# Cross-attention on one core: the raw context loaded as two column halves, each behind its own half of o, and issued ahead of the turn's store

## What is computed

```python
def layer(emb, latent, Wq, bq, Wk, bk, Wv, bv, gamma, beta):   # (32,224,512), (32,750,256)
    q = jnp.einsum('bte,ef->btf', emb, Wq) + bq
    k = jnp.einsum('bml,le->bme', latent, Wk) + bk
    v = jnp.einsum('bml,le->bme', latent, Wv) + bv
    w = jnp.einsum('bte,bme->btm', q, k) / sqrt(512)
    w = jax.nn.softmax(w, axis=1)                               # over the 224 rows t
    x = jnp.einsum('btm,bme->bte', w, v) + emb
    mu, var = mean(x, -1), var(x, -1)
    return (x - mu) * rsqrt(var + 1e-6) * gamma + beta
x = layer(x, ctx_512, L0 weights)
x = layer(x, ctx_512, L1 weights)
```

## Time and profile before

| | before |
|---|---|
| median of 3 runs | 1096.07 us |
| the profiled execution, its own time | 1094.51 us |
| its span, first to last instruction | 1092.7 us |
| PE matmul busy | 1024.3 us (94%) |
| PE weight load busy | 951.3 us (87%) |
| DVE busy | 869.1 us (80%) |
| ACT / POOL busy | 664.5 us (61%) / 564.8 us (52%) |
| mean granted TensorE clock | 0.974 |
| moved by DMA | 99.58 MB, 367054 packets, 91 GB/s |

### The profile page before, as it was taken

One profiled execution on the slowest core, in us unless ns is written; L12 is line 12 of the kernel. 1 busy time (PEld: TensorE's weight loads), 2 busy tenths in 40 slices (PEclk: granted clock), 3 DMA queues, 4 the chain that ended last, 5 costly groups with the idle time before them and its releaser, 6 DMA issues.

```text
span 1092.7 us, 24724 instructions
## 1 busy us (share of the span) xinstructions
PE 1024.3 (94%) x6984; PEld 951.3 (87%) x6984; DVE 869.1 (80%) x2593; ACT 664.5 (61%) x1873; POOL 564.8 (52%) x519
## 2 busy tenths in 40 slices
PE   6797999999999999999999999999999999999984
PEld 5677989988899898989989998989989899899973
DVE  2456888788888988888888888888888888888863
ACT  1325677566666765666667666666676566666743
POOL 0013465655546556555565565555655655456654
PEclk8688999999999999999999999999999999999997
DMA  7734344444444344443444444444444444344101
GB/s 144 169 78 82 78 95 96 90 93 93 89 97 100 92 95 84 99 102 76 100 98 93 91 89 97 96 83 98 100 93 94 83 101 104 78 102 98 46 18 34
DMA packets 367054, 99.58 MB, mean 91 GB/s; under 512 B 324833, under 2 KB 350881, under 8 KB 367009
## 3 DMA queue, kind: packets, MB, share of 16 engines
q1 hardware_dynamic: 364368, 99.02, 41.2%
q10 hardware_dynamic: 2640, 0.01, 0.2%
HBM read 84.29 MB, written 14.68 MB: 91 GB/s over the span
## 4 chain that ended last, share of the span: by engine, by line
PE 51%; DMA 17%; SPq 16%; issue 7%; DVE 3%; ACT 3%; POOL 2%; DVEq 0%; ACTq 0%; POOLq 0%
PE oq_bank L591 21%; DMA raw<-in_ctx_dram 14%; SPq L346 9%; SPq L347 5%; PE score_bank L567 4%; PE score_bank L568 4%; PE score_bank L572 4%; PE pv_bank L622 3%; DMA cb<-in_ctx_dram 3%; PE oq_bank L543 2%; PE oq_bank L538 2%; PE oq_bank L539 2%; PE pv_bank L618 2%; PE pv_bank L617 2%; ACT probs L749 2%
## 5 line engine op out<-in xcount | busy, mean ns | idle before, releaser
L591 PE MATMUL oq_bank<-probs,raw 125*128 125x224 f32 x1536 | 320.8, 359 | 21.9 <-DMA raw<-in_ctx_dram 16.6
L591 PEld LDWEIGHTS oq_bank<-probs,raw 125*128 125x128 f32 x1536 | 284.8, 193 | 29.9 <-DMA raw<-in_ctx_dram 22.0
L749 ACT ACTIVATE probs<-probs,neg_max 125x224 f32<-125x224 f32 x384 | 181.5, 476 | 178.4 <-DVE neg_max L959 178.3
L1142 POOL TENSOR_TENSOR psum<-probs 125x672 f32<-125x672 f32 x64 | 103.3, 1614 | 300.2 <-ACT probs L758 300.2
L567 PE MATMUL score_bank<-qT_hi,cT_hi 128*125 128x224 f32 x768 | 199.2, 286 | 3.1 <-ACT cT_hi L706 1.6
L568 PE MATMUL score_bank<-qT_hi,cT_lo 128*125 128x224 f32 x768 | 189.1, 273 | 0.0
L1185 POOL TENSOR_TENSOR y_out<-z,gamma_row 112x512 f32<-112x512 f32 x63 | 94.1, 1515 | 160.3 <-ACT z L782 160.3
L758 ACT ACTIVATE probs<-probs,rsum 125x224 f32<-125x224 f32 x384 | 154.0, 474 | 22.6 <-DVE rsum L967 22.6
L567 PEld LDWEIGHTS score_bank<-qT_hi,cT_hi 128*125 128x125 f32 x768 | 145.3, 189 | 9.4 <-issue 4.9
L959 DVE CUSTOM_DVE_ANT_0 probs<-score_bank,d_row 125x224 f32<-125x224 f32 x384 | 139.6, 382 | 15.8 <-PE score_bank L572 13.8
L572 PE MATMUL score_bank<-qT_lo,cT_hi 128*125 128x224 f32 x768 | 146.8, 273 | 0.0
(11 more groups left out here) (96 smaller groups left out, 2083.8 us busy)
## 6 DMA issues: line engine op xcount, KB each, us to landing
raw<-in_ctx_dram SPq DMA_DIRECT2D x32, 750.0 KB
cb<-in_ctx_dram SPq DMA_DIRECT2D x256, 92.0 KB
xb<-in_x_dram SPq DMA_DIRECT2D x512, 28.0 KB, 1.7
x<-in_x_dram SPq DMA_DIRECT2D x32, 448.0 KB, 3.6
out_dram<-y_out SPq DMA_DIRECT2D x31, 448.0 KB, 3.1
y<-in_L_xattn_Wq_dram SPq DMA_DIRECT2D x4, 512.0 KB, 8.3
cb<-in_ctx_dram SPq DMA_DIRECT2D x128, 3.5 KB
x<-in_L_xattn_Wk_dram SPq DMA_DIRECT2D x2, 512.0 KB, 9.8
```

Of the source, the lines that this page charges most:

```text
L591: ins = nc.tensor.matmul(o, raw[0:MP, u.slot, c, cols], probs[0:MP, u.par4, c, :], start=(c == 0), stop=(c == MC - 1))
L749: ins = act.activation(probs[0:MP, u.par4, c, :], probs[0:MP, u.par4, c, :], ACT.Exp, bias=neg_max[0:MP, u.par4, c:c + 1], scale=-1.0, acc ...
L1142: pool.tensor_tensor(psum3[0:MP, :, :], probs[0:MP, u.par4, 0:HALF, :], probs[0:MP, u.par4, HALF:MC, :], ALU.add).then_inc(psum3_done, 1)
```

## The change

The raw context of a batch is loaded by two transfers. Transfer l brings the columns `l*128:(l+1)*128` of every row (750 rows of 512 bytes each, where there were 750 of 1024), waits for the half l of o of b(-1) only, and increments a semaphore of its own. PE waits for half 0 ahead of `o_product(a(+0), 0)` and for half 1 ahead of `o_product(a(+0), 1)`. Both transfers are issued ahead of `store(b(-2))`, where the one of before came behind it.

```diff
-        raw_loaded = [sem("raw_loaded0"), sem("raw_loaded1")]
+        raw_loaded = [[sem("raw_loaded00"), sem("raw_loaded01")], [sem("raw_loaded10"), sem("raw_loaded11")]]
...
-            def load_ctx(u):
+            def load_ctx(u, l):
                 if not u.real:
                     return
                 if u.past(-4):
 
-                    sp.wait_ge(o_ready, u.n(-1, 2))
+                    sp.wait_ge(o_ready, u.n(-1, 2, l - 1))
                     sp.sem_inc(wait_alone, 1)
-                sp.dma_start(raw[0:MP, u.slot], ctx[u.batch()].rearrange("(c p) l -> p c l", c=MC)).then_inc(raw_loaded[u.slot], 16)
+                cols = slice(l * P, (l + 1) * P)
+                src = ctx[u.batch()].rearrange("(c p) l -> p c l", c=MC)
+                sp.dma_start(raw[0:MP, u.slot, :, cols], src[:, :, cols]).then_inc(raw_loaded[u.slot][l], 16)
...
-            load_ctx(start)
+            load_ctx(start, 0)
+            load_ctx(start, 1)
...
                 if a(+1).later(1):
                     load_x(a(+1))
+                if a(+0).later(0):
+                    load_ctx(a(+0), 0)
+                    load_ctx(a(+0), 1)
                 store(b(-2))
-                if a(+0).later(0):
-                    load_ctx(a(+0))
...
                 cols = slice(l * P, (l + 1) * P)
-                if u.layer == 0 and l == 0:
-                    pe.wait_ge(raw_loaded[u.slot], u.turns(16))
+                if u.layer == 0:
+                    pe.wait_ge(raw_loaded[u.slot][l], u.turns(16))
```

## The result

| | before | changed |
|---|---|---|
| median of 4 runs | 1096.28 us | 1054.16 us |
| lowest to highest | 1094.2 to 1100.38 | 1051.85 to 1057.63 |
| ratio, 95% interval | 1 | 0.9596 (0.9567 to 0.9625) |
| the profiled execution, time / span | 1094.51 / 1092.7 us | 1051.85 / 1049.8 us |
| mean granted TensorE clock in it | 0.974 | 0.979 |

The change is worth 42 us at the medians, where 30 were forecast. Run again later, beside fresh runs of the kernel before, the same kernel had a ratio of 0.9646 (0.9627 to 0.9665), 38 us.

What follows compares the result with a forecast made beforehand. PE bounds the kernel, with the raw load causing both its winnable stalls; 0.75 us for the raw wait plus 1.3 for earlier cb per pair, over 14.5 pairs, gives 30 us: 1064.5 profiled, 1066 us median, range 1053 to 1096.

Steps and rivals of the forecast that it cites:

- What bounds the kernel: PE, busy 1024.3 of 1092.7 us; its raw wait (21.3 us) and oT_lo wait at L622 (16.3) both come from the raw load.
- The raw wait: PE's wait at the first raw-context product: half 0 issued at R - 3.9, both halves in time, 21.3 us gone.
- R: The moment SyncE issues the raw load, or half 1 in the changed kernel; other times are counted from it in us.
- The price of the halves: DMA cost of doubled rows: 27 ns per 512 bytes, 150 rows on each of 5 engines, 4.1 us a half.
- When cb lands: In the DMA queue behind raw load and store: cb 0.55 to 2.05 us earlier, 1.3 taken as the middle.
- the store might only lie in line: Store between half 1 and cb: cb gains up to 2.05 us if not held, 0.55 if it waits the store's 1.5.
- full pace of the cb issues: Sign in SyncE's queue: cb issues back at two in 1.3 us by 6 to 7.3 us after half 1's issue, instead of 7.55.
- The sum: Per pair of turns, 1.3 us in the L622-stalled one plus 0.75 in the other, 2.05; times 14.5 pairs, 30 us.
- the cap: Most that a turn stalled at L622 can gain: 0.59 + 1.21 = 1.8 us; 1.34 a turn on average, 39 us in all.
- Rival B: Store does not hold cb and both PE stalls go: 39 us, 1057 us, or 1053 with pipeline fills; chance 0.25.
- C: Cb lands as late as now, so the raw stall only moves to L622: 3 us gained, 1093 us; chance 0.12.
- D: Slower because row count rules: cb up to 5 us late, up to some 130 us lost, 1123 us at 36 ns; chance 0.13.

Runs made afterwards that it cites:

- the halves together: Two half loads behind the store, both waiting for both halves of o, against the changed kernel's halves moved behind the store: 1120.84 us, 1.0301 of the kernel before.
- the whole load: As a run: the kernel before with its one whole raw load moved ahead of the store: 1125.35 us, ratio 1.0345.
- The quarters: The changed kernel with every half loaded as two quarters, rows of 256 bytes: 1071.29 us, 0.9785 of the kernel before.

## Why the prediction was wrong

**What bounds the kernel: right.** Both stalls led to the raw load. "Removing the raw wait alone would thus mostly move the stall to L622; what counts is when cb lands" is what the halves together showed: 21.3 us of raw wait gone, the stall at oT_lo up from 16.3 to 51.9.

**The raw wait: right.** Half 0 was issued at R - 3.9, as forecast, and the wait is gone in every turn.

**The price of the halves: the step that failed.** "27 ns for 512 bytes" was right as the share of an engine's time: a window of the changed kernel inside half 0 gives 0.36 x 16 / 213 rows per us = 27 ns (109 GB/s are 213 rows of 512 bytes):

```profile
443.00:445.00 2.00, 2.00 (x20) 1.99 (x19) 0.87 (x4) 1.39 (x4) 1.92 (x2) 1.00 0.36 109
```

But I multiplied it by 150 rows on each of **5** engines, while the same share of 0.36 x 16 counts 5.8 engines as busy. The rows pass at the measured rate, 5 / 213 per us = 23.5 ns on five engines. For the whole load I had taken the rate (750 KB at 121 GB/s, 6.35 us), for the halves the share; by one measure a half is 3.5 us and not 4.1. The Trainium skill's rule of 3 fixed cycles a descriptor besides one per 32 bytes ("DMA: Bandwidth & Descriptors", on why small descriptors are slow), applied to the whole load's 42 ns a row (121 GB/s on five engines), gives an estimated 23 ns for 512 bytes; the trace agrees (23.5).

**When cb lands: mis-sized through it.** With 3.5, half 1 ends at R + 1.65 + 3.5 = R + 5.15 instead of R + 5.95, and cb is 0.8 us earlier. The forecast's 0.55 to 2.05 becomes 1.35 to 2.85, and the measured gain at the last cb issue, 1.6 to 2.3 us (2.1 in the means), lies inside. "The middle, 1.3" fell short of the 1.8 at which the stalled turns stop gaining. The other assumption of that step, that the store might only lie in line, was too kind: with the whole load it held cb by 1.3 of its 1.5 us, with the halves by some 1 us.

The quarters are close to the case that the forecast had worked out: at their rate a half takes 4.2 us, for the 4.1 assumed. There cb came 0.9 us earlier, within 0.55 to 2.05, the stall at oT_lo stayed, and the forecast's sum with that gain, (0.9 + 0.75) x 14.5 = 24 us, stands against 0.81 x 29 = 23.5 measured. So this run bears out the rest of the working, and the size of the half is what failed.

One sign was off beyond that: full pace of the cb issues was to come back at R + 6 to 7.3 and came back at R + 3.65, when half 1 was by this working still under way. From there the 12 issues, held by nothing, take 8.85 us and set when cb is complete: in the five kernels where VectorE waits for cb, the hand-over comes 1.2 to 1.4 us after the last issue's end. That SyncE is held until the raw load has nearly drained fits the kernel before; why it was let go so early here stays open.

**The sum.** With the cap reached a stalled turn gains 1.8, and a pair 1.8 + 0.75 = 2.55, 37 us: measured 37.7. That they agree so well is partly luck: 3.4 us at oT_lo are still there in the window, 0.3 us in one turn of two, and 1.8 us of "issue", which was to stay, went with the rest. Rival B, to which I gave 0.25, described what happened, though its reason did not hold (the store does hold cb) and a small rest of the second stall is left. Its price was 1057, and 1053 with the pipeline fills.

**The range.** Its low end was B's best value with no room for the spread of the runs. The first 100 us vary by 5 us with the clock granted there, and the measured value slipped under it by 1 us. The interval of the ratio, 1048.6 to 1055.0 on 1096.07, reaches into the range, and the second measurement, 0.9646, gives 1057.3, inside it. So the 1 us is chance, but the forecast gain isn't made right by it: 37.7 us in the steady part for 30.

**The rivals C and D** did not come about, but their mechanism is real: with the halves together cb came 0.6 to 0.8 us later, and the kernel was 31 us slower, some 12 of them through the clock. Halving the rows was affordable because half 0 starts 3.9 us early; without that it loses.

## What to carry to other kernels

A load whose wait looks small (0.75 us a turn) can cost as much again through what is queued behind it on the same engines: follow the issue times of the next transfers, not only the waiting instruction. Before splitting or hurrying a load, look at its rate: 121 GB/s at a share of a third says that most engines don't take part, and cutting 125 partitions into 112 and 13 gave the same gain without any new order. When costing pieces of a transfer, use one measure for whole and part; the share and the rate differ by 15% for the rows of 512 bytes.

## What was not expected of the hardware

- The share of busy time counted for rows on five engines grows as they shorten: 0.34 at 1024 bytes, 0.36 at 512, 0.40 at 256, at 121, 109 and 91 GB/s. Quartering the rows costs a quarter of the rate.
- SyncE is held at an issue when a long raw load on five engines is still under way, though the mean share of all 16 is only 0.34 to 0.36: the store's issue took 2.20 us instead of 0.35, a pair of cb issues 3.92 instead of 0.93.
- After stalls of 2.3 to 2.8 us PE was granted 1.2 GHz for 3.5 us in eight turns of the kernel with the halves together, and in other turns with a stall as long it was not. A turn with the fall was 1.5 us longer than one without. No other profiled execution shows a fall in the steady part.
- The start of the kernel varies by 5 us between executions with the granted clock (0.70 or 0.91 between 40 and 60 us) at the same work; that is an eighth of the change's effect.
